# Graph attention with fewer rectified tiles, chosen by head, and with row maxima spread over a whole layer

## The reference, cut to what matters

```
h    = (x @ W).reshape(n, 4, 32);  al_s = (h * a_s).sum(-1);  al_d = (h * a_d).sum(-1)
e    = leaky_relu(al_s[src] + al_d[dst], 0.2)
m    = segment_max(e, dst);  ex = exp(e - m[dst])
out  = segment_sum(h[src] * ex / segment_sum(ex, dst)[dst], dst)
```

## Time and profile before

| | |
|---|---|
| median of 3 runs | 914.59 us (912.77 to 918.94) |
| profiled execution | 908.62 us, span of its trace 906.8 us |
| TensorE busy | 847.1 us, 93% of the span |
| VectorE busy | 663.7 us, 73% |
| ScalarE busy | 501.3 us, 55% |
| GpSimd busy | 290.4 us, 32% |
| chain that ended last | TensorE 78%, VectorE 14%, ScalarE 4% |

### The profile page before, as it was taken

The page is one execution under the profiler, slowest core; times in us unless marked ns, Lnnn a source line. Parts: engine busy times, 40 slices in busy tenths (PEclk is TensorE's granted clock), DMA queues, the critical chain, the costliest instruction groups (busy, mean ns, idle before and its releaser), DMA issues.

```text
span 906.8 us, 18692 instructions
## 1 busy us (share of the span) xinstructions
PE 847.1 (93%) x5480; PEld 544.3 (60%) x5514; DVE 663.7 (73%) x1788; ACT 501.3 (55%) x1007; POOL 290.4 (32%) x403
## 2 busy tenths in 40 slices
PE   8899959999999999999999898899899998899898
PEld 3657728989898989898989555222242324222244
DVE  6999986777777777777777476877687766878650
ACT  6432104666666666666666674556656665566531
POOL 8040047556555655555555100111031110111000
PEclk9999979999999999999999999999999999999999
DMA  3120032121212121212122100000000000000310
GB/s 88 40 80 1 0 140 63 53 70 51 70 53 70 49 72 53 70 58 71 46 70 54 39 1 1 1 0 1 1 1 0 1 1 0 1 1 0 143 44 23
DMA packets 19145, 35.87 MB, mean 40 GB/s; under 512 B 5280, under 2 KB 11552, under 8 KB 18976
## 3 DMA queue, kind: packets, MB, share of 16 engines
q0 software_dynamic: 7104, 19.41, 7.5%
q1 hardware_dynamic: 12000, 15.95, 5.0%
HBM read 29.56 MB, written 5.79 MB: 39 GB/s over the span
## 4 chain that ended last, share of the span: by engine, by line
PE 78%; DVE 14%; ACT 4%; issue 2%; POOL 1%; DMA 0%; DVEq 0%; ACTq 0%; POOLq 0%
PE PS L1466 9%; PE PS L1318 7%; PE PS L1231 7%; PE PS L1232 7%; PE PS L1312 5%; PE PS L1179 5%; PE PS L1250 5%; PE PS L1451 5%; DVE OHd L1014 5%; PE PS L1457 4%; PE PS L1224 3%; PE PS L1366 3%; PE PS L1237 3%; PE PS L1309 2%; PE PS L1417 2%
## 5 line engine op out<-in xcount | busy, mean ns | idle before, releaser
L407 POOL DMA_INDIRECT room<-Qtab,gidx x148 | 148.0, 1000 | 96.0 <-DVE gidx L840 61.1
L557 ACT ACTIVATE OHe<-OHs,sew 128x128 bf16<-128x128 bf16 x408 | 126.6, 389 | 33.0 <-DVE OHs L950 19.6
L1014 DVE CUSTOM_DVE_ANT_0 OHd<-PS,room 128x1024 bf16<-128x1024 f32 x96 | 112.3, 1220 | 8.6 <-PE PS L1417 8.5
L421 POOL TENSOR_SCALAR KV<-room,pid 128x256 bf16<-128x256 uint8 x74 | 73.8, 998 | 125.8 <-DVE MS L915 120.3
L568 ACT ACTIVATE m2s<-m2s 128x512 f32<-128x512 f32 x68 | 42.9, 630 | 93.1 <-DVE m2s L941 93.1
L459 POOL TENSOR_TENSOR zl<-AL,Sx 128x8 f32<-128x8 f32 x9 | 1.9, 213 | 264.3 <-DVE Sx L1014 264.3
L1231 PE MATMUL PS<-Wm,m1T 128*128 128x256 f32 x276 | 83.2, 383 | 0.0
L1232 PE MATMUL PS<-Wm,m1T 128*128 128x256 f32 x276 | 82.7, 382 | 0.0
L941 DVE TENSOR_TENSOR m2s<-PS,bm 128x512 f32<-128x512 f32 x68 | 47.0, 691 | 47.8 <-PE PS L1232 47.8
L955 DVE TENSOR_SCALAR OHd<-iotaN,dstf 128x1024 bf16<-128x1024 f16 x136 | 71.6, 566 | 7.9 <-PE PS L1318 7.9
L1318 PE MATMUL PS<-OHs,m2s 128*128 128x128 f32 x544 | 76.0, 282 | 0.0
(11 more groups left out here) (358 smaller groups left out, 1736.1 us busy)
## 6 DMA issues: line engine op xcount, KB each, us to landing
BT<-Wtab SPq DMA_DIRECT2D x1, 4096.0 KB, 12.6
room<-Qtab,gidx POOLq DMA_INDIRECT x148, 2.8
room<-Stab SPq DMA_DIRECT2D x1, 2048.0 KB, 10.4
Wtab<-H SPq DMA_DIRECT2D x4, 512.0 KB, 3.1
Wtab<-cs SPq DMA_DIRECT2D x4, 512.0 KB, 3.1
Qtab<-room SPq DMA_DIRECT2D x1, 1024.0 KB, 4.5
Wn<-in_L_gnn_Wn SPq DMA_DIRECT2D x1, 1024.0 KB, 5.2
x<-in_x SPq DMA_DIRECT2D x1, 512.0 KB, 4.1
```

Of the source, the lines that this page charges most:

```text
L407: g.indirect_dma_start(out=G[:, p % SLOTS, k, :], out_offset=None, in_=Qtab, in_offset=bass.IndirectOffsetOnAxis(ap=gidx[:, p, k:k + 1], a ...
L557: a.activation(OHe[:, k, j, :], OHs[:, k, :], ACT.Copy, scale=sew[:, j, bass.ds(2 * g + k, 1)])
L1014: v.tensor_tensor_reduce(junk[n % 2], bank(4, 2), mask[:, i, :], 1.0, 2 * FAR, ALU.subtract, ALU.max, Sx[:, i, hd:hd + 1]).then_inc(S("gat ...
```

## The change

It chooses the ramped units by head: units 1 and 3 of head 0, 1 and 6 of head 1, unit 1 of head 2 and none of head 3, five in a layer where there were nine. The maxima of heads 1 to 3 are one list, taken in order by the table MAXIMA, whose key is the unit number and whose value is how many are taken behind it: those of head 1 behind units 0 to 6, those of head 2 behind units 8 to 12, those of head 3 behind units 13 to 18. `source_row` of heads 2 and 3 moves by the table ROWS: head 2's from behind unit (0, 5) to behind (0, 6), head 3's from behind (1, 5) to behind (1, 4), each with a wait for all maxima of the head before. The division moves from behind unit 3 to behind unit 4.

```diff
-RAMPED = (1, 3, 5)
+RAMPED = ((1, 3), (1, 6), (1,), ())
+MAXIMA = {0: 1, 1: 2, 2: 3, 4: 1, 6: 1, 8: 3, 9: 2, 10: 1, 12: 2, 13: 2, 14: 1, 15: 1, 16: 1, 17: 2, 18: 1}
+ROWS = {(0, 6): 2, (1, 4): 3}
...
-        ramped = lambda n: n // NB % HEADS < HEADS - 1 and n % NB in RAMPED
+        ramped = lambda n: n % NB in RAMPED[n // NB % HEADS]
...
-                between = {0: (0, 1), 1: (2, 3), 2: (4, 5), 3: (6,), 4: (7,)}
+                taken = NB
                 for hd in range(HEADS):
                     for j in range(NB):
                         if not ramped(HEADS * NB * l + NB * hd + j):
                             sloped(hd, j)
-                        if hd + 1 < HEADS:
-                            for i in between.get(j, ()):
-                                greatest(hd + 1, i)
-                        if hd and j == 3:
+                        for _ in range(MAXIMA.get(NB * hd + j, 0)):
+                            greatest(*divmod(taken, NB))
+                            taken += 1
+                        if hd and j == 4:
                             divide(hd - 1)
...
-                        if j == 5 and hd + 2 < HEADS:
-                            eng.wait_ge(S("gat_smax"), HEADS * NB * l + NB * (hd + 2))
-                            source_row(hd + 2)
+                        if (hd, j) in ROWS:
+                            eng.wait_ge(S("gat_smax"), HEADS * NB * l + NB * ROWS[hd, j])
+                            source_row(ROWS[hd, j])
```

## The result

The changed kernel takes 893.88 us (median; 891.63 to 894.80) against 914.6 (912.77 to 918.94). The ratio is 0.9757, with a 95% interval from 0.9735 to 0.978. The forecast was 894 us, from 886 to 904.

A forecast was written before the change was run, and what follows sets the result against it. TensorE's own work was taken to bound the attention. Head terms of -1.5, -1.45, -3.3 and -0.6 us made -6.8 a layer, -20.5 over three, moving the median from 914.6 to 894 us, range 886 to 904.

The forecast's parts named there:

- TensorE's own work sets the pace: Attention: work taken from TensorE is worth its full time while VectorE stays in step; -6.8 us a layer.
- Head 0: First head of a layer: one unit less ramped, waits removed and added, about -1.5 us, to about 19.0.
- The wait of 0.87: TensorE's wait for VectorE at unit (0, 2): goes, since the sloped step starts 1.14 us earlier.
- the new one at unit 5: Head 0: TensorE waits for unit 5's sloped step, which needs the exponential of unit 3; +0.4 us.
- the one for GpSimd: Before `bound_row(1)`: two sloped steps hold up GpSimd's chain; between 0 and +0.9 us, +0.9 taken.
- The 0.16: Head 0: a later TensorE wait, counted as one for VectorE, goes as well; -0.2 us in the sum.
- Head 1: One unit less ramped, VectorE without slack, TensorE waits 0.27 before `source_row(3)`: -1.45 us, to about 19.9.
- Head 2: Two units less ramped; head 3's GpSimd chain ends 1.4 us before `bound_row(3)`: -3.3 us, to about 16.3.
- Head 3: Nothing ramped before or after; the division behind unit 4 removes TensorE's wait of 0.57: -0.6 us, to about 14.6.
- B: Rival: VectorE becomes the bound in head 1, its lead lost; -4.6 us a layer, 901 us, chance 0.20.
- C: Rival: head 3's GpSimd chain gets one instruction through per sloped step; -3.9 us a layer, 903 us, chance 0.06.
- E: Rival: TensorE's clock drops to 1.2 GHz in the attention; two heads of twelve would give 933 us, chance 0.04.

The follow-up runs named there:

- ramps alone: Kernel before with only the choice of ramped units new; maxima, source rows and division not moved: 931.66 us against 919.67, ratio 1.011.
- late sloped step: Changed kernel with VectorE's sloped step of unit (1, 0) behind the first maximum of head 2: layer 69.94 us, ratio to the kernel before 0.9781.
- division at 3: Changed kernel with the division back behind unit 3: layer 71.72 us, ratio to the kernel before 0.9836.
- ramps 1 and 5: Changed kernel with units 1 and 5 of head 1 ramped, not 1 and 6: layer 70.76 us, timed once.
- table alone: Changed kernel with units 1, 3 and 5 of heads 0 to 2 ramped as before: layer 76.62 us, ratio to the kernel before 1.0004.

## Why the prediction was right

- **TensorE's own work sets the pace.** This was true of the kernel before, and the sum held: -7.1 us a layer, forecast -6.8. But the runs show the condition to be narrower than I wrote. The same work taken away without the new order costs up to 4.0 us a layer; "for as long as VectorE, which takes it over, stays in step" carried the whole result.
- **Head 0**, forecast 19.0, took 18.8. The wait of 0.87 went, the new one at unit 5 is 0.32 (0.4), the one for GpSimd 0.65 (0.9). The chain took 4.6 us (4.8), and it is the two sloped steps that stretch it; of the two ends given, 0 and 0.9, the upper was nearer. The rule of the Trainium skill (SBUF — State Buffer, Who interferes with whom), that any GpSimd instruction that reads SBUF is blocked by a VectorE one with two SBUF inputs, agrees with the 1.15 us of a tensor_scalar here and the 1.14 of a cast in the kernel with the ramps alone.
- **One term of head 0 was no wait.** The 0.16 that the prediction took off stands at unit (0, 4), where the trace of before names no engine and has a record for only one of the two matmuls. It stands there again, with one record, in the first two layers of both repeats of the changed kernel. VectorE's third wait, of 0.16, is at unit (3, 2), also with one record. What was taken off too much was covered by 0.3 put on too much, for the waits at unit 5 and for GpSimd. This is the line (x1):

```profile
686.01 0.38 PE L1457 MATMUL PS<-rowA,sel 128*128 128x512 bf16 x1 [0.16 <-issue]
```

- **Head 1**, forecast 19.9, took 19.9. The wait before `source_row(3)` is 0.18 (0.27). VectorE without slack was right: the late sloped step, the division at 3 and the ramps 1 and 5 each made it later there and cost 1.1 to 1.3 us in this head.
- **Head 2**, forecast 16.3, took 16.2. The chain of head 3 was held four times and took 6.6 us; it ended at 724.4 and TensorE wanted it at 727.3, 2.9 us of margin instead of the 1.4 that I had.
- **Head 3**, -0.6, gave -0.63.
- **The rivals.** B did not come, but table alone shows it: 22.75 us in head 1, with VectorE waiting for a source row, the cause that I had named. The cause of C, and E itself, came with the ramps alone. I gave E 0.04 on the ground that no head would be busy less than 88%, and the changed kernel bears it out (17.15 of 18.81 us is the least of its heads, at full clock). With the ramps alone the clock fell behind waits of 2.47 us and less that this change avoids; that these brought it down is not shown.
- **The forecast of the median** rested on subtracting from it what the profiled execution saves. The median moved by 20.7 us, the attention by 21.4. That 893.88 fell so close to 894 is luck: the runs of each kernel in this comparison lie 3 to 6 us apart, the sum was 0.3 us a layer too small, and the profiled execution took 891.6 where 888.1 was forecast, because its first unit started 4.4 us later.

The expectations for ramps and table alone were wrong by 7 to 8 and by 1.6 us a layer, though made from the same prices. I worked those by sums over a head and not unit by unit; the changed kernel I had followed unit by unit. That this is why they failed is argued and not shown, though in both the error lies in waits of single units (1.09, 1.45 and 0.75; 0.87 and 0.75) that a sum over a head does not hold.

## What to carry to other kernels

When work moves from the bounding engine to one that is some 70% busy, as here, the sum over a stage can mislead: follow both engines step by step, with how far ahead the second may run (here two units) and what it needs from the first. Measure such a change in parts: here parts that gained nothing or lost alone won together. VectorE instructions with two SBUF inputs stretched a GpSimd chain of 2.8 us to 4.6, 6.6 and 8.3, so end such chains well before they are wanted, or start them where VectorE has an input in PSUM, as under the maxima. Count the records of a repeated step before reading a small gap ahead of it as a wait.

## What the runs showed that I had not expected

TensorE's clock fell to 1.2 GHz within the attention of the kernel with the ramps alone, for 1.1 us lost each time. It did so in the first two layers and not in the third. The wait for GpSimd ahead of it was 1.63 us in the first, 2.47 in the second and 2.47 in the third, and TensorE's other waits in head 2 are the same in all three to 0.1 us, missing records allowed for. The third layer:

```profile
850.00:855.00 5.00, 2.99 (x12) 0.52 (x12) 4.74 (x5) 1.87 (x2) 2.50 (x3) 1.00 0.00 0
855.00:860.00 5.00, 3.29 (x14) 0.52 (x12) 4.31 (x4) 2.58 (x3) 4.48 (x8) 1.00 0.00 0
860.00:864.00 4.00, 2.26 (x15) 0.82 (x16) 0.78 (x2) 1.82 (x3) 0.76 (x1) 1.00 0.00 0
```

What tells the layers apart, no run shows. And GpSimd, between two sloped steps that follow each other at 1.2 us, got one instruction through without making VectorE late: 2.48 us for both steps, where the pair before them, at 682.8 with no GpSimd instruction beside it, took 2.52.
